# One written list of stages for all eight batches in place of an opening, a repeated trip and a closing

## The reference, cut to what matters

```python
x = x + xattn(layernorm(x), ctx)           # 8 heads of 64, 64 context rows of 192
x = x + expert_ffn(layernorm(x))           # 16 experts of 64; sigmoid gates, the 4 largest
x = x + film_s4d(x, ctx)                   # per head the 32 largest scores, softmax, FiLM,
                                           # S4D long convolution through a DFT, FiLM, gelu FFN
x = x + expert_choice(x)                   # 8 experts, each takes its best 512 of 4096 rows
```

## Time and profile before

| | |
|---|---|
| median of 3 runs | 1468.9 us (1468.54 to 1472.57) |
| span of the profiled execution | 1470.0 us |
| PE busy | 1280.7 us, 87% |
| DVE busy | 925.6 us, 63% |
| ACT busy | 465.3 us, 32% |
| POOL busy | 325.8 us, 22% |

### The profile page before, as it was taken

How to read it: one execution, slowest core, us unless ns; L and a number is a source line. 1 busy time by engine, 2 the same in 40 slices (tenths; PEclk the granted TensorE clock), 3 DMA queues, 4 the chain that set the end, 5 groups by cost and what they waited for, 6 DMA issues and landing times. The chain is left out here.

```text
span 1470.0 us, 17444 instructions
## 1 busy us (share of the span) xinstructions
PE 1280.7 (87%) x5222; PEld 768.4 (52%) x5222; DVE 925.6 (63%) x3439; ACT 465.3 (32%) x837; POOL 325.8 (22%) x598
## 2 busy tenths in 40 slices
PE   4677968999999899899989989999887719999996
PEld 3444644465466455546545554645444516666764
DVE  6647789767767776865677786686987382211110
ACT  2544432042324315213431521343132433233221
POOL 3121221023112203201220320222102303332331
PEclk9677989999999999989999999999998858999999
DMA  9002000200300400030030003003000025453321
GB/s 293 9 15 59 18 1 22 51 18 15 88 18 1 102 18 1 25 79 18 1 102 17 1 16 87 16 2 87 7 1 1 30 93 173 109 145 87 90 37 18
DMA packets 44904, 72.51 MB, mean 49 GB/s; under 512 B 8101, under 2 KB 26760, under 8 KB 44682
## 3 DMA queue, kind: packets, MB, share of 16 engines
q1 hardware_dynamic: 38666, 62.87, 14.6%
q0 software_dynamic: 6144, 8.52, 3.3%
HBM read 58.27 MB, written 13.07 MB: 49 GB/s over the span
## 5 line engine op out<-in xcount | busy, mean ns | idle before, releaser
L773 POOL TENSOR_SCALAR ve<-mv 128x2 f32<-128x2 f32 x74 | 16.6, 225 | 552.9 <-DVE mv L1041 552.8
L1604 PE MATMUL ps<-x,keys 128*128 128x512 f32 x256 | 127.0, 620 | 0.5 <-DVE hT L1133 0.4
L1761 PE MATMUL ps<-hT,values 128*128 128x512 f32 x256 | 118.2, 592 | 0.0
L2189 PE MATMUL experts_ps<-experts_yT,experts_fc 128*128 128x512 f32 x256 | 111.9, 595 | 1.2 <-ACT experts_yT L2114 1.2
L2201 PE MATMUL experts_ps<-experts_fc,experts_hT 128*128 128x256 f32 x512 | 112.0, 379 | 0.8 <-ACT experts_hT L2126 0.8
L1604 PE MATMUL ps<-zT_second,w 128*128 128x512 f32 x224 | 102.3, 598 | 7.8 <-ACT big L1552 7.2
L2201 PEld LDWEIGHTS experts_ps<-experts_fc,experts_hT 128*128 128x128 f32 x512 | 96.6, 190 | 14.6 <-ACT experts_hT L2126 1.6
L1604 PE MATMUL ps<-w,big 128*128 128x256 f32 x448 | 98.9, 380 | 0.8 <-ACT big L1552 0.8
L2098 DVE SCALAR_TENSOR_TENSOR experts_o<-experts_ps,experts_wh,experts_b2w 128x256 f32<-128x256 f32 x32 | 15.5, 484 | 128.7 <-PE experts_ps L2201 128.7
L2126 ACT ACTIVATE experts_hT<-experts_ps,experts_b 128x512 f32<-128x512 f32 x64 | 44.0, 687 | 155.4 <-PE experts_ps L2189 155.4
L1604 PEld LDWEIGHTS ps<-w,big 128*128 128x128 f32 x448 | 84.3, 190 | 13.8 <-ACT big L1552 1.6
(11 more groups left out here) (435 smaller groups left out, 2489.7 us busy)
## 6 DMA issues: line engine op xcount, KB each, us to landing
gT<-expert_gates SPq DMA_DIRECT2D x16, 1024.0 KB, 9.6
experts_fc<-in_fc1T SPq DMA_DIRECT2D x8, 1024.0 KB, 5.2
experts_fc<-in_fc2T SPq DMA_DIRECT2D x8, 1024.0 KB, 8.7
xT<-in_xT SPq DMA_DIRECT2D x8, 512.0 KB, 3.5
x<-in_x SPq DMA_DIRECT2D x8, 512.0 KB, 3.5
expert_table<-tb SPq DMA_DIRECT2D x7, 528.0 KB, 7.6
out_x<-x SPq DMA_DIRECT2D x7, 512.0 KB, 6.9
w<-in_W SPq DMA_DIRECT2D x2, 1024.0 KB, 9.4
```

The costliest lines, as they stand in the source:

```text
L773: nc.gpsimd.tensor_scalar(o, i, c, None, ALU.add).then_inc(*tick(*event))
L1604: last = nc.tensor.matmul(o, l, r_, start=start, stop=stop)
L1761: last = nc.tensor.matmul(bank("O2", k), S["values"][:, c, k * P:(k + 1) * P], hT[:, c % RING, :], start=(c == 0), stop=(c == HC - 1))
L2189: last = nc.tensor.matmul(g_bank(m), fc1[e % 3][:, k, m * P:(m + 1) * P], yT[e % 2][:, k, :], start=(k == 0), stop=(k == DC - 1))
```

## The change

The three lists become one, `SCHEDULE`, with the batch written out in each entry, and `take` loses its `trip`. It holds the same 940 stages, each once, in another order; no part of a stage, no wait, bank, buffer or DMA is changed. Between the two, 108 of POOL's 154 parts keep their position in the order of their engine, 192 of DVE's 541, 165 of ACT's 377 and 187 of PE's 421. The core of the diff, with the start, the stretch around the gates of batches 2 and 3, and the end:

```diff
-OPENING = [
-    (KERN, 0, "steps", 0), (ATTEND, 0, "keys", 0), (KERN, 0, "centre", 0), (KERN, 0, "steps", 1), (KERN, 0, "centre", 1),
-    (KERN, 0, "means"), (KERN, 0, "phases", 0), (KERN, 0, "powers", 0), (KERN, 0, "phases", 1), (ATTEND, 0, "keys", 1), (KERN, 0, "masks"),
...
-    (ATTEND, 0, "soften", 3), (ATTEND, 0, "attend", 2), (ATTEND, 0, "attend", 3), (ATTEND, 0, "soften", 4), (KERN, 0, "bias"),
-    (ATTEND, 0, "attend", 4), (KERN, 0, "powers", 1), (KERN, 0, "phases", 3), (ATTEND, 0, "attend_out"), (ATTEND, 0, "route"),
...
-    (KERN, 0, "phases", 4), (MID, 0, "mlp", 1), (KERN, 0, "film_row"), (KERN, 0, "powers", 3), (KERN, 0, "centre", 5), (MID, 0, "mlp", 2),
...
-ORDER = [
...
-    (LAST, 0, "scores", 0), (ATTEND, 2, "gates", 0), (MID, 1, "pick", 3, 3), (ATTEND, 2, "gates", 1), (MID, 1, "text", 2),
-    (ATTEND, 2, "gates", 2), (ATTEND, 2, "gates", 3), (LAST, 0, "scores", 1), (MID, 1, "picked", 0), (LAST, 0, "shift_scores"),
-    (MID, 1, "weigh"), (LAST, 0, "route_experts"), (MID, 1, "picked", 1), (LAST, 1, "film_in", 0), (ATTEND, 2, "spread"),
-    (LAST, 1, "film_in", 1), (MID, 2, "relu", 0), (MID, 2, "mlp", 0), (LAST, 1, "film", 0), (MID, 2, "relu", 1), (LAST, 0, "table"),
-    (LAST, 1, "fold"), (MID, 2, "relu", 2), (LAST, 1, "turn"), (MID, 2, "relu", 3), (MID, 2, "mlp", 1), (LAST, 1, "product", 0),
-    (LAST, 1, "product", 1), (MID, 2, "relu", 4), (LAST, 1, "film", 1), (LAST, 1, "transform"), (MID, 2, "text", 0),
-    (LAST, 1, "product", 2), (MID, 2, "relu", 5), (LAST, 1, "product", 3), (MID, 2, "mlp", 2), (MID, 2, "relu", 6), (LAST, 1, "unfold"),
...
+SCHEDULE = [
+    (KERN, 0, "steps", 0), (KERN, 0, "steps", 1), (ATTEND, 0, "keys", 0), (KERN, 0, "centre", 0), (KERN, 0, "centre", 1),
+    (KERN, 0, "means"), (ATTEND, 0, "keys", 1), (KERN, 0, "phases", 0), (KERN, 0, "powers", 0), (KERN, 0, "centre", 2),
+    (KERN, 0, "phases", 1), (KERN, 0, "centre", 3), (KERN, 0, "masks"), (ATTEND, 0, "keys", 2), (KERN, 0, "phases", 2),
+    (ATTEND, 0, "norm"), (ATTEND, 0, "soften", 0), (ATTEND, 0, "attend", 0), (KERN, 0, "bias"), (ATTEND, 0, "attend", 1),
...
+    (ATTEND, 0, "spread"), (ATTEND, 0, "gates", 3), (KERN, 0, "phases", 4), (KERN, 0, "film_row"), (KERN, 0, "centre", 5),
+    (KERN, 0, "powers", 3), (MID, 0, "relu", 0), (KERN, 0, "fold_film"), (MID, 0, "relu", 1), (MID, 0, "mlp", 2), (KERN, 0, "phases", 5),
...
+    (KERN, 0, "powers", 4), (MID, 0, "text", 0), (MID, 0, "mlp", 6), (MID, 0, "relu", 5), (KERN, 0, "phases", 6), (MID, 0, "mlp", 7),
+    (MID, 0, "relu", 6), (MID, 0, "relu", 7), (MID, 0, "mlp", 8), (MID, 0, "mlp", 9), (KERN, 0, "powers", 5), (ATTEND, 1, "keys", 0),
+    (ATTEND, 1, "keys", 1), (MID, 0, "mlp_out"), (ATTEND, 1, "norm"), (MID, 0, "text", 1), (KERN, 0, "phases", 7),
...
+    (LAST, 0, "norm_out", 0), (LAST, 0, "ffn_add", 1), (LAST, 0, "norm_out", 1), (MID, 1, "pick", 3, 2), (LAST, 0, "scores", 0),
+    (ATTEND, 2, "attend_sum"), (MID, 1, "picked", 0), (LAST, 0, "scores", 1), (ATTEND, 2, "route"), (ATTEND, 2, "gates", 0),
+    (ATTEND, 2, "turn_route"), (MID, 1, "pick", 3, 3), (ATTEND, 2, "gates", 1), (ATTEND, 2, "gates", 2), (ATTEND, 2, "gates", 3),
+    (MID, 1, "picked", 1), (LAST, 0, "route_experts"), (MID, 1, "text", 2), (LAST, 0, "shift_scores"), (LAST, 1, "film_in", 0),
+    (LAST, 1, "film_in", 1), (MID, 2, "mlp", 0), (LAST, 1, "film", 0), (ATTEND, 2, "spread"), (MID, 2, "mlp", 1), (LAST, 1, "film", 1),
+    (LAST, 0, "table"), (MID, 2, "relu", 0), (MID, 2, "relu", 1), (MID, 2, "relu", 2), (MID, 2, "text", 0), (LAST, 1, "fold"),
+    (LAST, 1, "transform"), (LAST, 1, "turn"), (LAST, 1, "product", 0), (MID, 2, "text", 1), (MID, 2, "relu", 3), (MID, 2, "mlp", 2),
...
+    (MID, 3, "mlp", 0), (MID, 2, "picked", 1), (LAST, 2, "film_in", 0), (MID, 3, "mlp", 1), (LAST, 1, "table"), (LAST, 2, "film_in", 1),
+    (MID, 3, "relu", 0), (MID, 3, "relu", 1), (ATTEND, 3, "spread"), (LAST, 2, "film", 0), (LAST, 2, "fold"), (LAST, 2, "film", 1),
+    (LAST, 2, "transform"), (MID, 3, "mlp", 2), (MID, 3, "relu", 2), (LAST, 2, "turn"), (MID, 3, "mlp", 3), (LAST, 2, "product", 0),
...
+    (LAST, 7, "norm_out", 0), (LAST, 7, "ffn_add", 1), (LAST, 7, "scores", 0), (LAST, 7, "norm_out", 1), (LAST, 7, "scores", 1),
+    (LAST, 7, "route_experts"), (LAST, 7, "shift_scores"), (LAST, 7, "table"),
 ]
...
-FULL_FROM, FULL_TO = 0, 3
-
-def take(stages, order, trip=0):
+def take(stages, order):
 
-    for phase, plus, name, *t in order:
+    for _, b, name, *t in order:
         if name in stages:
-            stages[name](trip + plus, *t)
+            stages[name](b, *t)
...
         def trips(eng, stages):
 
-            take(stages, OPENING)
-            for b in range(FULL_FROM, FULL_TO):
-                take(stages, ORDER, b)
-            take(stages, CLOSING)
+            take(stages, SCHEDULE)
```

284 lines of the change are left out of this document (158 added, 126 removed).

## The result

The changed kernel takes 1475.1 us (median of 9 runs, 1471.64 to 1478.08) against 1468.9 us (9 runs, 1467.23 to 1472.66): ratio 1.0037 [1.0025, 1.005], some 5.4 us slower. The forecast was 1463, faster.

A forecast was written before the change was run, and what follows sets the result against it. TensorE bounds the middle; in the opening TensorE and VectorE wait for each other. 1470.0 - 10.0 (opening) + 3.1 (middle) + 1.1 (tail) = 1464.2, median 1.1 lower: 1463; range 1447 to 1477, the forecast's own 1456 to 1468.

The forecast's parts named there:

- (a): Opening: K0.steps/1 ahead of keys/0 and centre/0 on ScalarE removes VectorE's 6.0 us wait; 2.5 us gained (0 to 6.0).
- (d): Opening: batch 0's picks and shift ahead of powers/6 on VectorE, keys/2 among them; 2.5 us gained of a 6.7 gap.
- (b): Opening: `bias`, 4.77 us of TensorE work, moves ahead of attend/1, where TensorE waits for the softmax; 3 us gained.
- (c): Opening: centre/5 moves ahead of powers/3, into the 8.9 us gap; 2 us gained (0 to 4.5).
- The gates loop: Batches 2 to 6, attend_out to mlp/2: idle up 7.5 us, clock loss down 4.4, net +3.1 (-9.6 to +14).
- The 16.5 us: Least time from the start of `spread` to mlp/2, through copy, DMAs and relu/0, whatever TensorE does in between.
- Rest of the batch: From mlp/2 to ffn_out, walked for batches 1 to 4: no TensorE wait over 0.5 us added or removed; 0.
- the tail: Last batch: gelu/6 ahead of film gains 0.7, route_experts (1.85 us) lands on the path; +1.1 us (-1 to +2).
- batch 7's loop: Batch 7's `spread` also has less work behind it before mlp/2; 3 us, counted only in the middle's upper end.
- B: Slower rival: gates loop becomes the bound at mlp/2 of batches 2 to 6; 1480 or 1477; chance 0.25.
- A: Rival: the order hides the gates loop, middle gives -9.6 and opening 14; 1445; chance 0.13.
- C: Rival: nothing comes out, VectorE near full, TensorE's gain handed back at the `kernel` parts; 1468; chance 0.20.

The follow-up runs named there:

- e2: New order for the first 193 entries (to about 318 us), old order after, against the kernel before: 1464.4 us, ratio 0.9967.
- e1: Old order written out as one list, same instructions in the same order as the kernel before: 1470.8 us, ratio 1.0003.
- e3: Old order with entries 193 to 832 (about 318 to 1035 us) in the new order, against the kernel before: 1478.4 us, ratio 1.0047.
- e9: Old order with entries 193 to 745 (batches 2 to 6) in the new order, against the kernel before: 1467.6 us, ratio 0.9982.
- e4: Old order up to entry 832 (about 1037 us), new order from there, against the kernel before: 1475.8 us, ratio 1.0039.
- e10: Old order with entries 745 to 832 (batch 7's attention and mlp) in the new order, against the kernel before: 1479.6 us, ratio 1.006.
- e13: New order up to entry 745 (opening and batches 2 to 6), old order behind, against the kernel before: 1465.3 us, ratio 0.998.
- e14: As e10, but M7.relu/0 put back behind L5.norm_out/1 on VectorE; against the kernel before: 1476.7 us, ratio 1.0052.
- e15: New order up to entry 832 with M7.relu/0 back behind L5.norm_out/1, old order from there, against the kernel before: 1468.9 us, ratio 0.9993.
- e11: Old order with entries 832 to 863 (first half of the last part) in the new order, against the kernel before: 1477.3 us, ratio 1.0044.
- e12: Old order with the entries from 863 on in the new order, against the kernel before: 1475.0 us, ratio 1.0034.
- e17: Old order with entries 745 to 832 new on all engines but VectorE, against the kernel before: 1475.2 us, ratio 1.0035.
- e18: Old order with entries 745 to 832 new on VectorE alone, against the kernel before: 1478.7 us, ratio 1.0057.
- e16: Old order with only M7.relu/0 moved ahead of L5.norm_out/1 on VectorE, against the kernel before: 1480.2 us, ratio 1.0067.

## Why the prediction was wrong, point by point

**The opening: right in sign, about half the size.** 10.0 us forecast, 8.0 in the profiles, 4.8 in the runs (e2; its interval reaches from 2.8 to 7.1). Of the four terms (a) was sized too small: taken at 2.5, it brought 5.4 at powers/0. ACT's work at `means` is only 2.0 earlier, but DVE's wait at 23 us is gone and its `phases` 0 starts 6.0 earlier (23.95 against 29.93). (d) took 2.0 from the wait before powers/6 (6.73 to 4.70). For (b) and (c) the waits in front of powers/1 and powers/3 stand as before. I had not walked `keys` 1 into the 19.2 us wait, nor batch 1's own loop: attend_out to mlp/2 grew from 30.3 to 34.3 us there and gave back 4.

**The gates loop: half of the idle time, and a sum that met by luck.** The 16.5 us held within 0.4 (16.2 to 16.9 in five batches). Idle PE in the five stretches rose by 3.6 (25.0 to 28.6 from the windows), forecast 7.5. PE's busy time stayed (129.1 and 129.0) with some 4.5 us more work in the stretches, so the clock gave back about as much, forecast 4.4; one minus the clock times the lengths, which counts idle time too, fell from 15.4 to 13.7. That the stretches are 3.5 us longer, forecast 3.1, is no hit: they hold more work, and executions of one order differ by nearly as much (154.1 in before, 156.6 in e1's profile; 157.6 for the new one again in e3's). The blocks in front of mlp/2 were 3.9, 0, 3.2, 1.8 and 3.8 us against 4.7, 7.2, 3.8, 4.6 and 4.7, since part of the cover ran at the lower clock and so covered longer: batch 3's stretch has 0.78. The Trainium skill ("TensorE: Matmul & The Clock Gate", section "HAM oscillation — how this bites in real kernels") tells of matmul bursts that each wait for a transfer and then start cold. The trace agrees in batches 2 and 6 (2.80 and 2.93 us for four matmuls) and not in batches 4 and 5 (1.98 behind an idle 3.24 and 1.78), so not every block pays the upper price that this rule would give it.

**Rest of the batch at 0: wrong by a little, and walked too short.** Batches 2 to 6 as a whole gain 2.6 us (e9). In the two profiles PE's idle time in the middle stretch, outside the five loops, falls from 11.1 to 7.3 us. But I walked it for batches 1 to 4 only and carried the zero to batch 7.

**The end: the step that failed.** Two terms of the sum were too small: the tail, +1.1, and batch 7's loop, which stands in the sum with nothing and only in an upper bound with 3 us. By the runs the last part costs 5.7 us by itself (e4), batch 7's part 8.8 by itself (e10), and the new order behind entry 745 costs 8.3 in the changed kernel (from e13's -2.9 to +5.4).

In the tail it was the price of gelu/6 that failed. I read it as 0.69 us of ACT that go out of the way, a gain of 0.7. It is also 1.88 us of PE work, and in the old order that work covered the time until DVE had made what film/1 needs. In the new order PE stands idle there for 1.81 us, and film/1 and `transform` take 3.69 and 6.56 us instead of 1.98 and 3.72. The other move, route_experts, was forecast at +1.85; putting it back returns 0.9, near what the runs can tell.

In batch 7's loop it was the zero that failed. `spread` has no spare time before mlp/2 in the new order (16.2 us in e14, against 21.5 in e1 and 19.8 in before), and relu/0 stands in DVE's queue before its gates are there, with L5.norm_out/1 behind it and PE's scores/1 behind that (idle 3.10 us against 1.52). The page of before had it in view: relu/0 at the earlier trace rows is a DVE wait on a DMA, and whatever is put behind such a wait inherits it. In the two profiles 2.7 of the 10.2 us lie up to mlp/9. By the lists and the durations the new order has some 2.8 us less PE work there (L5.gelu/5 stands ahead of attend_out, M7.text/1 behind mlp/9), so for like work it is some 5.5. How much of the loss in the changed kernel is this part's is not settled: it costs 8.8 in the old list (e10), and 1.9 behind the new stages with relu/0 put back (e15 against e13).

**The rivals.** B named the right kind of wait, but not the place where it costs: PE stands idle in front of mlp/2 in four of batches 2 to 6, and these batches do not lose; in batch 7 the gates are late through DVE's queue. Its 1477 to 1480 is nearer to 1475.1 than the forecast, but by luck: it took the five blocks at the full clock loss, batch 7 at 3, and nothing for the tail. A did not come: the blocks are there. C's reason does not hold: the opening's gain was not handed back at the `kernel` parts; with 2.8 of the middle it reaches 960 us as 10.8.

**What stays open.** The parts do not add. Batch 7's part and the last part cost 8.8 and 5.7 by themselves (e10, e4), but 8.3 together in the changed kernel; e11 and e12 cost 11.5 apart and 5.7 together, e17 and e18 13.5 apart and 8.8 together. All fourteen profiles with any new piece behind entry 745 take 209.3 to 214.5 us from attend_out to `table`, all six with the old order there 204.3 to 206.1. The waits that open in front of film, scores/1, mlp/2 and `spread` are read from the traces; no run of the new order took away only these, so that they make the whole loss is argued and not shown. Why the clock falls behind some of them and not behind others is not settled.

The best version run is e2, the new opening with the old rest: 0.9967.

## What to carry to other kernels

In an in-order queue price a moved wait by what stands behind it, not by the instruction that waits: exchanging two neighbours on VectorE cost 9.8 us, eight times the 1.2 us that the first one waited. When a list is reordered, walk the last repetition by itself; it has no next batch to fill the gaps, and a zero carried over from the steady batches is not a result. Before a stage is moved, look up its part on every engine: gelu/6 was priced by its copy on ScalarE, and its matmuls were what kept TensorE busy. Time the pieces of a reordering separately before taking the whole: here a gain of 4.8 us in the opening was hidden under a larger loss at the end.

## What the hardware showed that was not expected

A wait of about a microsecond more in front of dense matmuls was followed by several microseconds at the lower clock level: 1.36 and 1.19 us idle (e14, e17) and then four matmuls at 3.68 instead of 1.88; 2.71 instead of 1.52 (e16) and then 0.60 instead of 0.90 over 17 us. The 1.52 us wait in before and e1 had no sequel of that size, and 3.24 us in batch 4 of the kernel after had none. So the length of a gap alone did not tell what follows it.

Executions of one order differ in where the clock falls. e1 runs the instructions of before in the same order; in its profile M4.mlp/2 ends 3.7 us earlier than in before's (640.6 against 644.3), and batch 5's loop takes 35.5 us instead of 30.9. Twelve runs of e13 lie between 1458.31 and 1473.41, and runs of the kernel before beside them between 1462.14 and 1474.98: with one profile of each, a difference of 5 us could not have been told from this scatter. The search and the experts, behind `table`, are the same in all twenty kernels, and in their profiles they take 294.1 to 297.2 us: in e1 the mean granted clock from 1205.1 to 1235.1, where the experts begin, was 0.75 (294.1 us), in e16 from 1211.3 to 1241.3 it was 0.62 (297.1 us).
